# x turned by block loads and a VectorE block transpose, with the first layer norm folded into centred weights

## The reference, cut to what matters

```python
def _layernorm(x): return (x - mean(x)) / sqrt(var(x) + 1e-5)       # over the last axis, 256

# x: (8, 1024, 256) float32; wq, wk, wv: (64, 256); wo: (256, 64)
def attn(x):
    Q, K, V = x @ wq.T, x @ wk.T, x @ wv.T
    energy  = K^T V                    # 64 x 64, summed over the 1024 tokens of one batch
    return (Q @ energy) * sqrt(3/64) @ wo.T

def ffn(x):                            # W_fc: (1024, 256), W_proj: (256, 1024)
    y = square(relu(x @ W_fc.T)) @ W_proj.T
    return spike_count(y) / 5          # 5 steps of a leaky integrator with threshold 1

x = x + attn(_layernorm(x))
x = x + ffn(_layernorm(x))
```

## Time and profile before

| | |
|---|---|
| median of 3 runs | 506.89 us (506.52 to 507.18) |
| the profiled execution | 509.51 us; its span from first to last instruction 507.7 us |
| mean granted TensorE clock | 0.984 of full speed |
| busy share of the span | PE 96%, PEld 87%, DVE 69%, ACT 56%, POOL 41% |
| DMA | 19.6 MB, queue q1 busy for 10.4% of 16 engines' span |
| step 0 | 26.1 us |
| a step of the loop | 29.0 to 29.3 us |

### The profile page before, as it was taken

The page is one execution under the profiler, slowest core; times in us unless marked ns, Lnnn a source line. Parts: engine busy times, 40 slices in busy tenths (PEclk is TensorE's granted clock), DMA queues, the critical chain, the costliest instruction groups (busy, mean ns, idle before and its releaser), DMA issues.

```text
span 507.7 us, 9333 instructions
## 1 busy us (share of the span) xinstructions
PE 487.9 (96%) x3124; PEld 441.4 (87%) x3124; DVE 351.6 (69%) x991; ACT 284.9 (56%) x519; POOL 208.0 (41%) x171
## 2 busy tenths in 40 slices
PE   6979799999999999999999999999999999999995
PEld 6768689898999998999999988999998999999995
DVE  5476457777777857777887776778777774939447
ACT  2526665656565565656556565655656575646540
POOL 2353344354344434434443533444343543445340
PEclk9889899999999999999999999999999999999998
DMA  8111001010111111011111101111100101010102
GB/s 290 71 43 41 1 1 43 21 63 2 43 41 43 44 43 41 1 41 41 42 41 41 42 0 44 41 41 41 42 0 0 41 1 43 0 43 2 42 1 83
DMA packets 5792, 19.63 MB, mean 39 GB/s; under 512 B 640, under 2 KB 1280, under 8 KB 5504
## 3 DMA queue, kind: packets, MB, share of 16 engines
q1 hardware_dynamic: 5760, 19.27, 10.4%
HBM read 10.88 MB, written 8.39 MB: 38 GB/s over the span
## 4 chain that ended last, share of the span: by engine, by line
PE 86%; DVE 7%; issue 4%; ACT 2%; DMA 1%; POOL 0%; DVEq 0%; ACTq 0%; POOLq 0%
PE hid_ps L739 11%; PE hid_ps L740 11%; PE hid_ps L741 11%; PE y_ps L741 11%; PE y_ps L739 11%; PE y_ps L740 11%; PE work_ps L779 3%; PE work_ps L764 2%; DVE stat L523 2%; PE kv_ps L739 2%; PE kv_ps L740 1%; PE kv_ps L741 1%; PE work_ps L845 1%; PE work_ps L846 1%; PE work_ps L739 1%
## 5 line engine op out<-in xcount | busy, mean ns | idle before, releaser
L312 POOL TENSOR_TENSOR hid_l<-hid,hid_h 128x512 fp32r<-128x512 f32 x128 | 165.6, 1298 | 258.4 <-ACT hid_h L363 258.4
L352 ACT ACTIVATE relu<-hid_ps 128x512 f32<-128x512 f32 x128 | 76.6, 599 | 123.9 <-PE hid_ps L741 123.9
L741 PE MATMUL y_ps<-wdn_h,hid_l 128*128 128x256 f32 x480 | 135.7, 283 | 0.0
L740 PE MATMUL y_ps<-wdn_l,hid_h 128*128 128x256 f32 x480 | 135.6, 283 | 0.0
L739 PE MATMUL y_ps<-wdn_h,hid_h 128*128 128x256 f32 x480 | 135.2, 282 | 0.0
L739 PE MATMUL hid_ps<-x2T_h,wup_h 128*128 128x512 f32 x256 | 107.1, 418 | 0.6 <-DVE x2T_l L576 0.3
L740 PE MATMUL hid_ps<-x2T_l,wup_h 128*128 128x512 f32 x256 | 100.8, 394 | 0.0
L741 PE MATMUL hid_ps<-x2T_h,wup_l 128*128 128x512 f32 x256 | 100.6, 393 | 0.0
L740 PEld LDWEIGHTS y_ps<-wdn_l,hid_h 128*128 128x128 f32 x480 | 91.3, 190 | 4.9
L739 PEld LDWEIGHTS y_ps<-wdn_h,hid_h 128*128 128x128 f32 x480 | 91.3, 190 | 4.9
L741 PEld LDWEIGHTS y_ps<-wdn_h,hid_l 128*128 128x128 f32 x480 | 91.3, 190 | 0.0
(11 more groups left out here) (116 smaller groups left out, 636.5 us busy)
## 6 DMA issues: line engine op xcount, KB each, us to landing
xs<-x_dram SPq DMA_DIRECT2D x15, 512.0 KB, 3.3
out_dram<-x SPq DMA_DIRECT2D x15, 512.0 KB, 2.7
hid<-w_up_dram SPq DMA_DIRECT2D x1, 1024.0 KB, 7.3
x<-w_down_dram SPq DMA_DIRECT2D x1, 1024.0 KB, 9.3
xs<-x_dram SPq DMA_DIRECT2D x2, 256.0 KB, 4.1
out_dram<-x SPq DMA_DIRECT2D x1, 256.0 KB, 2.0
out_dram<-x SPq DMA_DIRECT2D x2, 128.0 KB, 1.9
wkv_raw<-w_kv_dram SPq DMA_DIRECT2D x1, 128.0 KB, 5.4
```

The source lines that it names most:

```text
L312: nc.gpsimd.tensor_tensor(hid_l[:, i % 2, c, :], hid[:, c % 4, :], hid_h[:, i % 2, c, :].bitcast(f32), ALU.subtract).then_inc(hid_ready, 1)
L352: nc.scalar.activation(relu[:, c % 2, :], hid_ps[c % 2][:, :], ACT.Relu).then_inc(relu_done, 1)
L740: mm(dst, a[0], b[1], start=False, stop=False)
L741: return mm(dst, a[1], b[0], start=False, stop=stop)
```

## The change

- **x is turned without TensorE, from group 3 on.** SP loads each group a second time into a new tile `x_block`, by eight DMAs (four partition blocks of 32 by two halves of the columns), each a box of 32 x 16 runs of 32 floats (128 bytes). One DVE instruction (`turn_blocks`) transposes all blocks of 32x32 of `x_block` into `x2n`, which is then x turned. Groups 0 to 2 are still turned by PE, now from `xs`.
- **The first layer norm is folded.** The mean goes into the weights: PE multiplies them by a matrix of 1/256 (`average_weights`), DVE subtracts the result (`centre_weights`). The deviation is put in later: on kv by a new DVE product (`kv_scale`, into `kv_scaled`, which ACT and DVE then split), and on attention inside `residual`, now four instructions of 256 columns in the place of two of 512.
- **Gone:** `normalise` of the first norm (four DVE instructions a group), the tile `xn`, `turn_first` from group 3 on.
- **Moved:** the high half of the turned x on ACT from c = 4 to c = 1, now read from SBUF; its low half from DVE to POOL from group 4 on, ahead of the low half of hidden piece c = 2. `normalise` of the second norm also waits until the turned x in `x2n` has been split.
- **Prologue:** w_kv is loaded first; `keep_warm` has other counts (9, 2, 2, 2, 8, 2 rounds before; 4, 8, 4, 2, 16, 4 now, four transposes each); moments of group 2 move from the prologue into step 0.

The diff, cut to its core:

```diff
+    x_blocks = x.rearrange("(g b q t) (k i e) -> g i k q t b e", b=4, q=32, t=TILES, k=EC, i=4)
...
+            def load_blocks(r, n):
+                if not isinstance(r, int) or n > BY_MATMUL:
+                    sp.wait_ge(x_turn, upto(r, n - BY_MATMUL))
+                for i in range(4):
+                    for k in range(EC):
+                        dst = x_block[32 * i:32 * (i + 1), k * GROUP:(k + 1) * GROUP]
+                        sp.dma_start(dst.rearrange("q (t b e) -> q t b e", t=TILES, b=4), x_blocks[r * UNROLL + n, i, k])\
+                            .then_inc(x_block_loaded, 16)
...
             def step(r, i):
+                if there(r, i + RING) and not (isinstance(r, int) and i < 0):
+                    load_blocks(r, i + RING)
                 if there(r, i + RING + 1):
                     load(r, i + RING + 1)
...
+            def x_low_half(r, n):
+                for k in range(EC):
+                    pool.wait_ge(xT_high, upto(r, n, EC, k + 1))
+                    last = nc.gpsimd.tensor_tensor(xT_l[:, n % 2, k, :], x_turned(r, n, k),
+                                                   xT_h[:, n % 2, k, :].bitcast(f32), ALU.subtract)
+                last.then_inc(xT_ready, 1)
...
             def kv_high_half(r, n):
-                act.wait_ge(kv_turned, upto(r, n + 1))
+                act.wait_ge(kv_in_scale, upto(r, n + 1))
...
+            def kv_scale(r, n):
+                dve.wait_ge(kv_turned, upto(r, n + 1))
+                dve.wait_ge(rstd_ready[0], upto(r, n + 1))
+                if there(r, n - 1):
+                    dve.wait_ge(kv_ready, upto(r, n))
+                by_token = rstd1[:, n % RING, :].unsqueeze(2).broadcast_to([P, TILES, 2 * HEAD])
+                nc.vector.tensor_tensor(kv_scaled[:, :].rearrange("p (t d) -> p t d", t=TILES),
+                                        kv_bank(r, n)[:, :].rearrange("p (t d) -> p t d", t=TILES),
+                                        by_token, ALU.mult).then_inc(kv_in_scale, 1)
...
             def residual(r, n):
-                for k in range(2):
-                    cols = slice(k * 512, (k + 1) * 512)
-                    last = nc.vector.tensor_tensor(x1[:, n % RING, cols], work_ps[k][:, :], xs[:, n % RING, cols],
-                                                   ALU.add)
+                for t in range(TILES):
+                    cols = slice(t * EMB, (t + 1) * EMB)
+                    att = work_ps[t // 2][:, (t % 2) * EMB:(t % 2 + 1) * EMB]
+                    last = nc.vector.scalar_tensor_tensor(x1[:, n % RING, cols], att, rstd1[:, n % RING, t:t + 1],
+                                                          xs[:, n % RING, cols], ALU.mult, ALU.add)
...
+            def turn_blocks(r, n):
+                dve.wait_ge(x_block_loaded, counted(r, BLOCK_LOADS * (n - BY_MATMUL + 1), BLOCK_LOADS * UNROLL))
+                dve.wait_ge(x2n_turned, upto(r, n - 2))
+                nc.vector.transpose(x2n[:, :], x_block[:, :]).then_inc(x_turn, 1)
...
             def first_step():                                # DVE
-                normalise(0, 2, 0)
-                xnT_low_half(0, 2)
-                first_moments(0, 3)
+                turn_blocks(0, 3)
+                xT_low_half(0, 2)
+                first_moments(0, 2)
+                xT_low_half(0, 3)
                 residual(0, 1)
                 moments(0, 1, 1)
+                q_low_half(0, 2)
+                kv_scale(0, 2)
                 kv_low_half(0, 2)
-                normalise(0, 3, 0)
-                q_low_half(0, 2)
-                normalise(0, 1, 1)
-                xnT_low_half(0, 3)
+                normalise(0, 1)
                 x2T_low_half(0, 1)
+                first_moments(0, 3)
+                kv_scale(0, 3)
                 kv_low_half(0, 3)
...
             def step(r, i):                                  # DVE
                 if there(r, i + 3):
+                    turn_blocks(r, i + 3)
                     first_moments(r, i + 3)
...
                 if there(r, i + 3):
+                    kv_scale(r, i + 3)
                     kv_low_half(r, i + 3)
```

More of the change, by code:

```diff
@@ L104, in build @@
         kvT = sb("kvT", [P, GROUP])
+        kv_scaled = sb("kv_scaled", [P, GROUP])
+        x_block = sb("x_block", [P, EC * GROUP])
         kv = sb("kv", [P, TILES, 2, 2, HEAD], f32r)
@@ L121, in build @@
         ve = [sb(f"ve{n}", [P, TILES]) for n in (1, 2)]
[L122 removed]
+        rstd1 = sb("rstd1", [P, RING, TILES])
+        rstd2 = sb("rstd2", [P, TILES])
         neg_half = sb("neg_half", [P, TILES])
@@ L458, in step @@
                             eo_high_half(r, i + 2)
-                    if c == 4 and there(r, i + 3):
-                        xnT_high_half(r, i + 3)
+                    if c == 1 and there(r, i + 3):
+                        xT_high_half(r, i + 3)
                     if c == 6 and there(r, i + 3):
@@ L750, in turn_first, with average_weights, turn_second @@
             def turn_first(r, n):
[L752 removed]
+                if n == 2:
                     pe.wait_ge(x2T_ready, 1)
[L755 to L757 removed]
+                for t in range(TILES):
+                    if n:
+                        pe.wait_ge(x_loaded[n], 16)
+                    elif t % 2 == 0:
+                        pe.wait_ge((first_pair_loaded, x_loaded[0])[t // 2], 16)
+                    for k in range(EC):
+                        at = t * EMB + k * P
+                        last = nc.tensor.transpose(turn_banks(n)[k][:, t * P:(t + 1) * P], xs[:, n, at:at + P], ident[:, :])
+                last.then_inc(first_x_turn, 1)
+            def average_weights(loaded, raw, first):
+                pe.wait_ge(loaded, 16)
+                for k in range(EC):
+                    last = mm((y_ps[0], e_ps)[first][:, 0:2 * HEAD], averager[:, :], raw[:, k * 2 * HEAD:(k + 1) * 2 * HEAD],
+                              start=(k == 0), stop=(k == EC - 1))
+                last.then_inc(mean_done, 1)
+            def turn_second(r, n):
                 for t in range(TILES):
                     if t % 2 == 0:
[L761 to L776 removed]
+                        pe.wait_ge(x2n_ready, upto(r, n, 2, t // 2 + 1))
                     for k in range(EC):
@@ L941, in step @@
                         attend(r, i + 1)
-                    if c == 4 and there(r, i + 3):
-                        turn_first(r, i + 3)
                     if c == 6 and there(r, i + 3):
```

188 lines of the change are left out of this document (98 added, 90 removed).

## The result

| | before | after |
|---|---|---|
| median of 20 executions each | 506.89 us | 502.99 us |
| lowest and highest | 504.70 to 508.95 | 500.61 to 506.98 |
| after / before | | 0.992, 95% interval 0.9903 to 0.9937 |
| the profiled execution (span) | 509.51 (507.7) | 501.43 (499.5) |

The change wins 3.9 us in medians, 8.1 between the two profiled executions. The forecast was 6.2 us (500.7), with 493 to 509 for the range.

The account below looks back on a forecast made before the run. PE was taken to bound the kernel, busy for 96% of the span. The terms -10.4 - 5.8 - 0.2 + 6.8 + 3.4 = -6.2 took 506.9 to 500.7 us; forecast band 497 to 503, 8-in-10 range 493 to 509.

Parts of the forecast that it names:

- Turning x off PE: Steps 1 to 12: eight PE transposes of 0.87 us a step go, 10.4 us won in all.
- The transpose, T = 1.2: DVE, ahead of the energy: the new block transpose takes 1.2 us a step.
- kv later, d = 1.0: DVE, low half of kv: two SBUF reads make it wait for POOL, so kv ends 1.0 us later.
- Waits at `energy_times_wo`: PE waits for DVE's late energy: 0.8 us in steps 3, 7, 11, 3.3 in 5 and 9; costs 6.8 us.
- The clock behind the longer waits: PE runs at half clock behind the two 3.3 us waits, steps 5 and 9: 1.7 us each, 3.4 in all.
- Step 0, 5.8 us won: Step 0 shrinks from 26.1 to 20.3 us, including 1.3 us for the second norm of group 1.
- Prologue, 0.2 won: Step 0 starts 0.2 us earlier, with `turn_second` later but at the higher clock; bounds 2 us either way.
- Hidden work: `kv_scale`, four-part `residual`, POOL's low halves, ACT's moved high halves and block loads (5 to 12 us a group) cost no time.
- B: Rival: DVE is less late for the energy, transpose plus kv delay 1.35 us; 496.6 us, chance 0.22.
- C: Rival: DVE's block transpose takes two passes, 2.5 us, so PE waits longer for the energy; 512.3 us, chance 0.08.
- D: Rival: the block loads' 128-byte runs bound the kernel, from 90 ns a run on; about 650 us, chance 0.11.
- E: Rival: other waits move in (DVE in step 0, POOL in the second norm, prologue); 503 to 509 us, chance 0.11.

Follow-up runs that it names:

- e8: Changed kernel with DVE's block transpose and first moments moved behind the energy, and three prologue `keep_warm` counts changed: 489.23 us, ratio 0.9641.
- e3: Changed kernel with the loop over steps 2 to 9, not 1 to 12, so no branch lies ahead of a closing step: 495.60 us, ratio 0.9766.
- e5: Kernel before, with DVE's first moments moved behind the energy and `normalise` of the first norm behind the low half of eo: 504.62 us, ratio 0.9946.
- e10: e8 with one more POOL wait in step 0, so that `normalise` of group 1 runs alone: 488.09 us, ratio 0.9630.
- e7: Changed kernel with the prologue's `keep_warm` counts of the kernel before: 502.47 us, ratio 0.9901.
- e6: Changed kernel with the low half of the turned x on DVE, not POOL: 503.91 us, ratio 0.9936.
- e12: e8 with the low half of the turned x on DVE, not POOL: 489.53 us, ratio 0.9664.
- e11: e8 with every block load done twice, the second after the first has landed: 489.19 us, ratio 0.9654.
- e4: Changed kernel with every DVE block transpose done twice into the same tile: 512.13 us, ratio 1.0095.

## Why the prediction was right, and where its terms were off

Point by point, first in the profiled executions (507.7 to 499.5, 8.2 us less where the forecast had 6.2):

- **Turning x off PE, 12 x 0.87 = 10.4: right.** From one `turn_second` to the next a step of the loop that is not closing takes 28.01 us after and 28.89 before, 0.88 less. The sign that the prediction named, 28.4 us for such a step, was wrong: 28.4 is what a closing step takes where PE doesn't wait (28.43 in e8).
- **The transpose, T = 1.2: right.** 1.228 to 1.245 us in all 13, and DVE's next instruction starts 1.16 later. 64 KB of blocks landed in 2.5 us. The factor of 19 that the Trainium skill (VectorE: DVE Perf Modes, The three transpose paths) gives for a copy that transposes by its access pattern is against the DMA's own hardware transpose, which no run here has; the prediction's 63 us took it times a plain load, which the page doesn't state. No run here tried single elements.
- **kv later, d = 1.0: mechanism right, size too large.** From `turn_second` on, the spikes behind the low half of kv start after 5.87 us in step 3 before (118.84 to 124.71) and after 6.65 in step 3 after (112.08 to 118.73): d = 0.78. The low half of kv lasted 1.02 in the place of 0.69, and POOL, which had started its second low half at about 117.0, was through at 118.26. The Trainium skill (SBUF — State Buffer, Who interferes with whom) says that VectorE with two SBUF inputs contends with a GpSimd instruction that reads SBUF, and calls the shared ports an exclusive lock. Were it blocked until POOL was through, it would have ended at 118.95; it ended at 118.80, so the trace agrees to 0.15 us, on the short side. The forecast added a full 0.69 behind POOL's end in just that way.
- **`ve`: right.** 0.17 in the place of 0.70.
- **Waits at `energy_times_wo`, 6.8 us: 5.8.** T + d was 1.16 + 0.78 = 1.94, not 2.2. In step 3 PE came to `energy_times_wo` 14.38 us after `turn_second` before (118.84 to 133.22) and 14.94 after (112.08 to 127.02); from one `turn_second` to the next steps 3, 7 and 11 took 29.09 to 29.11 us, 0.66 more than in e8 (28.44), where there is no such wait (0.8 forecast). Behind the branches it waited 2.99 and 2.97 (3.3 forecast), 1.9 more than before: 3 x 0.66 + 2 x 1.9 = 5.8. The arithmetic with 2.49 of branch, 0.53 and 0.86 held. A small wait in step 1 (0.25, with which the step is 0.5 longer than in e8) was missed.
- **The clock behind the longer waits, 3.4 us: the mechanism right, the size a matter of chance.** The profile lost 1.5 us, none behind the first wait. Over the executions the mean seems larger: e3, which shortens these waits to 0.4, wins 7.8 us by the ratios, of which 5.2 are waits. The same wait of 3 us cost 0, 1.5 and 2.6 us in the rows above. The step that failed is "half speed for 2.7 to 4.1 us costs 1.4 to 2.0; I take 1.7 for each": it made one value of what differs between executions.
- **Step 0, 5.8 us won: 4.6, or 2.6 against e5.** It took 21.5 us, not 20.3. The failed step is "I take 1.3 us for that": the path through the inverse deviation was named rightly, but `normalise` behind it was taken at its undisturbed time. It met POOL, took 3.4 us and not 1.38, and PE waited 1.05. e10 gives 1.34 back and with it 20.14, near the 20.3 of the forecast. The other side of the difference was off too: the 26.1 of before held some 2 us of lost clock that the 24.13 of e5, the same code, did not. The contention that I weighed for kv stood in the same profile for `normalise`: its instructions average 602 ns in the earlier trace rows, where four alone take 1.38 us.
- **Prologue, 0.2 won: 0.94,** inside the bounds of 2 us either way, but not by the prediction's reason. The 64 transposes took 6.99 us (27.59 to 34.58) and not 7.84, and e7 shows that the new counts cost more than they gave: with those of before, step 0 starts at 37.00. Against the 36.09 of e5 the new prologue is 1.5 us later.
- **Hidden work: right.** e6 and e12 show it for POOL's low halves of x, e11 for the 60672 packets and their issue. SP took 0.59 us for one issue and 5.3 to 7.4 for eight, not 0.4 each, and a packet 12.6 ns, below the 18 to 47 taken. `kv_scale` and `residual` (1.66 for four) had no run of their own; no wait of PE names them.

Summed: -10.4 - 4.6 - 0.9 + 5.8 + 0.5 for step 1 + 1.5 = -8.1.

**From the profile to the median.** Of the 2.6 us between profile and median the prediction said that it "is taken to be the same in both kernels". That assumption failed: the profile of before held more lost clock than its median (behind 1.93, 3.13 and 3.23 us of waiting), and e5 shows the same 3.23 us with no loss at all; the profile of after held less than its median. The two distances, 2.6 and 1.6 us, are what separates 8.1 from 3.9. Most of it lies ahead of step 1, which starts at 64.67 in the profile of before, at 60.22 in that of e5 and at 59.13 after: prologue and step 0 together are worth 5.5 us against one execution and 1.1 against the other. The forecast of 500.7 lies 2.3 us below the median of 502.99 as the sum of terms that were too dear by 2 us in the profile and an assumption that was worth 4.2 the other way: right in sign, range and the main mechanism (DVE late for the energy), with a centre that is nearer than its parts by luck. The median lies at the very edge of the forecast's own band of 497 to 503.

**The rivals.** B (T + d = 1.35) fell at 1.94. C was imitated by e4 and came at 4.8 us of its 5.4. D was refuted by e11. E was real in one of its named places, DVE in step 0.

## What to carry to other kernels

Work that is taken off the bounding engine is worth its time only if what it is put on isn't late for that engine somewhere: look for the one instruction in a step that the bound waits for, and put everything that nobody waits for behind it. Here 3.2 us of DVE work, moved behind the energy, brought three times the gain of the change itself. An idle time on the helper (a loop's branch) costs nothing until such an instruction stands right behind it.

## What the runs showed of the hardware that I had not expected

- **Equal waits, unequal clocks.** Behind a PE wait of 3.0 to 3.2 us the granted clock stayed at 1.00, or was 0.50 for 3.4 us (304.8 to 308.2 in the kernel after), or for 6.9 (185.0 to 191.9 in e6), at a cost of 0, 1.5 or 2.6 us; the first two stand in one execution. What decides it was not tested. The kernels with such waits and 12 to 20 executions (before, after, e5, e6) scatter by 4 to 6 us, those without (e8 to e12, five or six executions) by about 2. But e4, with waits of 4.3 and 4.4 us, scatters by 2.9 and e7 by 2.1, over six executions each, so the waits alone don't make the scatter.
- **A DVE instruction with a single SBUF tensor waits for POOL as well.** `normalise` (TENSOR_SCALAR, f32, SBUF to SBUF) takes 1.38 us for four alone and 3.42 beside two POOL subtractions. The Trainium skill (SBUF — State Buffer, Who interferes with whom) names `tensor_scalar` among those that can, in a two-port mode; no run here shows the mode. The prediction used only the rule for two SBUF inputs.
- **DVE at a loop's branch** idles 2.5 us in one layout of the program and not at all in another that differs by one unrolled step. What decides it was not tested.
- **128-byte runs are cheap enough:** 12.6 ns a packet of one DMA engine's time, by the doubled loads of e11.
